# Placing the last edge rows in full columns: 26 scatters of 128 rows and one of 64, where there were 32 of 106

## Time and profile before

| | us |
|---|---|
| timed runs, median of 3 | 4679.84 (4676.11 to 4682.98) |
| profiled execution: span from first to last instruction | 6104.5 |
| GpSimd busy | 3187.4 (52% of the span) |
| TensorE busy | 3504.6 (57%) |
| VectorE busy | 2563.8 (42%) |
| ScalarE busy | 1503.7 (25%) |
| mean granted TensorE clock | 0.746 of full speed |

### The profile page before, as it was taken

One profiled execution on the slowest core, in us unless ns is written; L12 is line 12 of the kernel. 1 busy time (PEld: TensorE's weight loads), 2 busy tenths in 40 slices (PEclk: granted clock), 3 DMA queues, 4 the chain that ended last, 5 costly groups with the idle time before them and its releaser, 6 DMA issues.

```text
span 6104.5 us, 83728 instructions
## 1 busy us (share of the span) xinstructions
PE 3504.6 (57%) x18191; PEld 1755.8 (29%) x18192; DVE 2563.8 (42%) x7891; ACT 1503.7 (25%) x3741; POOL 3187.4 (52%) x3191
## 2 busy tenths in 40 slices
PE   5377777777777777776324544345365345455347
PEld 2133333333333333333101222112132112222136
DVE  6266666666666666666330020131120021120368
ACT  3133333323323232322211111111111112111158
POOL 2455555555555555555376555645625635626720
PEclk8588888878888887888656676667666667667679
DMA  5333333333333333333123444334324334324256
GB/s 181 93 77 81 81 78 78 77 80 77 77 77 80 77 77 78 80 77 71 38 93 135 145 146 131 119 112 145 107 79 144 111 132 146 108 79 156 79 200 237
DMA packets 593641, 646.86 MB, mean 106 GB/s; under 512 B 423668, under 2 KB 430418, under 8 KB 587261
## 3 DMA queue, kind: packets, MB, share of 16 engines
q1 hardware_dynamic: 374705, 459.40, 23.2%
q0 software_dynamic: 101760, 110.75, 9.2%
q10 hardware_dynamic: 117068, 75.50, 4.1%
HBM read 451.74 MB, written 190.23 MB: 105 GB/s over the span
## 4 chain that ended last, share of the span: by engine, by line
PE 35%; issue 21%; another core or an unknown queue 21%; DVE 10%; DMA 8%; ACT 2%; POOL 2%; DVEq 1%; SPq 0%; ACTq 0%; POOLq 0%
PE bank L1742 10%; PE bank L1743 7%; PE bank L1823 6%; PE bank L1747 6%; DMA ld_all<-adjacency 3%; DMA rel_table<-ld_all 2%; DMA rel_and_z<-adjacency 1%; DVE hid_T L1305 1%; DMA ld_all<-l_sorted 1%; POOL l_sorted L711 1%; DVE hid_T L1326 1%; DVE hid_T L1584 1%; PE bank L1939 1%; PE bank L1771 1%
## 5 line engine op out<-in xcount | busy, mean ns | idle before, releaser
L711 POOL DMA_INDIRECT l_sorted<-arena,l_pos x1504 | 1539.2, 1023 | 1339.3 <-ACT arena L854 877.4
L686 POOL DMA_INDIRECT ld_all<-rel_table,rel_and_z x1564 | 1545.8, 988 | 1133.0 <-remote 503.2
L1742 PE MATMUL bank<-hid_T 128*128 128x400 f16 x2346 | 965.7, 412 | 672.6 <-issue 539.8
L1743 PE MATMUL bank<-hid_T 128*128 128x384 f16 x2346 | 940.5, 401 | 44.3 <-issue 43.5
L1326 DVE TENSOR_SCALAR hid_T<-count_key,hid_T 128x400 f16<-128x400 int16 x2346 | 592.1, 322 | 754.5 <-remote 526.7
L1823 PE MATMUL bank<-rel_and_z,ld_all 128*128 128x512 fp8e4 (+1 forms) x1872 | 522.3, 414 | 602.9 <-issue 534.1
L1823 PE MATMUL bank<-ld_all 128*128 128x512 fp8e4 (+1 forms) x1950 | 511.4, 420 | 337.4 <-issue 138.4
L1747 PE MATMUL bank<-ld_all,arena 128*32 x4692 | 527.1, 250 | 123.3 <-issue 121.3
L1742 PEld LDWEIGHTS bank<-hid_T 128*128 x2346 | 255.9, 109 | 1157.3 <-issue 1153.9
L774 ACT CAST ld_all<-bank 128x400 fp8e4<-128x400 f32 x391 | 191.1, 489 | 1551.6 <-remote 999.7
L1266 DVE COPY accT<-bank 128x512 f32<-128x512 f32 (+1 forms) x78 | 51.1, 656 | 1215.4 <-remote 797.1
(11 more groups left out here) (289 smaller groups left out, 4103.0 us busy)
## 6 DMA issues: line engine op xcount, KB each, us to landing
ld_all<-adjacency SPq DMA_DIRECT2D x72, 1600.0 KB
rel_and_z<-adjacency SPq DMA_DIRECT2D x72, 1600.0 KB
l_sorted<-zeros SPq DMA_DIRECT2D x147, 424.0 KB
arena<-in_edge_attr SPq DMA_DIRECT2D x195, 256.0 KB
ld_all<-l_sorted SPq DMA_DIRECT2D x33, 1277.5 KB, 6.0
adjacency<-ld_all ACTq DMA_DIRECT2D x391, 100.0 KB
rel_table<-ld_all SPq DMA_DIRECT2D x49, 520.0 KB, 3.6
ld_all<-rel_table,rel_and_z POOLq DMA_INDIRECT x1564
```

Of the source, the lines that this page charges most:

```text
L686: pool.indirect_dma_start(ring[:, c % RING, 0:TW], None, rel_table, bass.IndirectOffsetOnAxis(ap=rel_i[:, c:c + 1], axis=0)).then_inc(s(f" ...
L711: pool.indirect_dma_start(l3_sorted, bass.IndirectOffsetOnAxis(ap=l3_pos[0:parts, n * SB_K + k:n * SB_K + k + 1], axis=0), rows16[q][0:par ...
L1742: pe.matmul(b0[:, 0:w0], low[:, 0:P], pair_hot[q % 2][:, k, 0:w0], start=k == 0, stop=k == CG - 1)
L1743: pe.matmul(b1[:, 0:GW - w0], low[:, P:2 * P], pair_hot[q % 2][:, k, 0:GW - w0], start=k == 0, stop=k == CG - 1)
```

## The change

The rest of 3392 rows is laid out as 26 full columns of 128 rows (3328 rows, 26 per partition) and one column with the last 64 rows on 64 partitions. It is scattered by 27 indirect DMAs (`REST_DMAS`). The two loads of this rest, that of its source indices (by SyncE at the start) and that of its features (by ScalarE), become two loads each: one of 128 partitions and one of 64, of 4 bytes and of 192 bytes per partition. The waits on them count one more, and SyncE's wait for the scatters of the last block counts 27. Copies and splits still treat 32 columns. `block_in` loses a case that it never met.

```diff
-SB_REST = (E - NSB * SB) // SB_K
+REST_K = (E - NSB * SB) // P
+REST_TAIL = E - NSB * SB - REST_K * P
+REST_DMAS = REST_K + 1
...
-            sp.dma_start(l3_pos[0:SB_REST, NSB * SB_K:n_cols], A["src"][NSB * SB:E].rearrange("(p k) -> p k", k=SB_K)).then_inc(s("l3_src_loaded"), 16)
+            rest = slice(NSB * SB, NSB * SB + REST_K * P)
+            sp.dma_start(l3_pos[:, NSB * SB_K:NSB * SB_K + REST_K], A["src"][rest].rearrange("(p k) -> p k", k=REST_K)).then_inc(s("l3_src_loaded"), 16)
+            sp.dma_start(l3_pos[0:REST_TAIL, NSB * SB_K + REST_K:NSB * SB_K + REST_DMAS], A["src"][NSB * SB + REST_K * P:E].rearrange("(p k) -> p k", k=1),
+                         allow_slow_non_contiguous=True).then_inc(s("l3_src_loaded"), 16)
...
                 for q in range(3):
-                    sp.wait_ge(s(f"l3_moved{q}"), 16 * SB_K * (len(range(q, NSB + 1 - EARLY, 3)) + (q < EARLY)))
+                    last = (NSB - EARLY) % 3 == q
+                    sp.wait_ge(s(f"l3_moved{q}"), 16 * SB_K * (len(range(q, NSB - EARLY, 3)) + (q < EARLY)) + (16 * REST_DMAS if last else 0))
...
                 for m in range(NSB + 1 - EARLY):
                     n = m + EARLY
-                    parts, q = P if n < NSB else SB_REST, m % 3
+                    q = m % 3
...
-                    for k in range(SB_K):
+                    for k in range(SB_K if n < NSB else REST_DMAS):
+                        parts = REST_TAIL if n == NSB and k == REST_K else P
                         pool.indirect_dma_start(l3_sorted, bass.IndirectOffsetOnAxis(ap=l3_pos[0:parts, n * SB_K + k:n * SB_K + k + 1], axis=0),
                                                 rows16[q][0:parts, k, :], None).then_inc(s(f"l3_moved{q}"), 16)
...
-                act.wait_ge(s(f"l3_in{m % 3}"), m // 3 * 16 + 16)
+                act.wait_ge(s(f"l3_in{m % 3}"), m // 3 * 16 + (16 if m + EARLY < NSB else 32))
...
                 if block <= NSB:
-                    parts = P if block < NSB else SB_REST
                     act.wait_ge(s("l3_split"), n + 1)
-                    act.dma_start(ea_in[n % 3][0:parts, :, :],
-                                  A["edge_attr_48"][block * SB:block * SB + parts * SB_K, :].rearrange("(p k) d -> p k d", k=SB_K)).then_inc(s(f"l3_in{n % 3}"), 16)
+                    cols = SB_K if block < NSB else REST_K
+                    act.dma_start(ea_in[n % 3][:, 0:cols, :],
+                                  A["edge_attr_48"][block * SB:block * SB + P * cols, :].rearrange("(p k) d -> p k d", k=cols)).then_inc(s(f"l3_in{n % 3}"), 16)
+                    if block == NSB:
+                        act.dma_start(ea_in[n % 3][0:REST_TAIL, REST_K, :], A["edge_attr_48"][NSB * SB + REST_K * P:E, :]).then_inc(s(f"l3_in{n % 3}"), 16)
...
-            v.wait_ge(s("l3_src_loaded"), 32)
+            v.wait_ge(s("l3_src_loaded"), 48)
```

More of the change, by code:

```diff
@@ L66 @@
 ZERO_DMAS = -(-NBK * CAPC * WL // (2 * ZERO_W))
-assert SB_REST * SB_K == E - NSB * SB and NSB == NG // TG and NSB % 3 == 0 and CAP < FRONT
+assert 0 < REST_TAIL < P and REST_K < SB_K and NSB == NG // TG and NSB % 3 == 0 and CAP < FRONT
 assert PIECES == AHEAD_Z + 4 * (NG // TG) and FULL - PIECES * 8 == 2
@@ L537, in block_in @@
                 n = m + EARLY
-                parts = P if n < NSB else SB_REST
-                sp.dma_start(ea_in[m % 3][0:parts, :, :],
-                             A["edge_attr_48"][n * SB:n * SB + parts * SB_K, :].rearrange("(p k) d -> p k d", k=SB_K)).then_inc(s(f"l3_in{m % 3}"), 16)
+                sp.dma_start(ea_in[m % 3], A["edge_attr_48"][n * SB:(n + 1) * SB, :].rearrange("(p k) d -> p k d", k=SB_K)).then_inc(s(f"l3_in{m % 3}"), 16)
             for a in range(6):
```

## The result

The changed kernel took 4649.8 us (median of 4, 4644.9 to 4652.2), the kernel before on the same occasion 4681.4 (4 runs, 4676.1 to 4685.1): a ratio of 0.9932 with a 95% interval of 0.9918 to 0.9946, or 31.6 us less, between 25 and 38. Forecast were 4655 and 25.1 less, with a gain of 19 to 27 in the main case.

A forecast was written before the change was run, and what follows sets the result against it. GpSimd was taken to set the pace of the timed runs, its last scatter block delaying the last stage; 59.4 us of scatters became 34.3, other parts nothing, so 4679.8 - 25.1 = 4655, range 4650 to 4664.

The forecast's parts named there:

- main case: The forecast itself: shorter last scatter block saves 19 to 27 us, giving 4653 to 4661 us; chance 0.76.
- 1.27 a column: GpSimd's price of a 128-row scatter with its 0.30 us pause, against 1.855 for 106 rows; assumed for 64 rows too.
- 34.3, gain 25.1 on the path: Last scatter block on GpSimd: 59.4 us go, 33.0 and one 64-row scatter come, making 34.3, gain 25.1.
- replay: Last block replayed in the profile's placement, under VectorE's chain: loads at 5823, 22 us sooner, or 19 with a gap.
- GpSimd is nearly always busy: Six adjacency passes in timed runs: GpSimd works 4582 us, leaving about 98 for waits, so TensorE waits for it.
- the last block starts after VectorE has finished: End of the passes in timed runs: VectorE done within 60 to 78 us, GpSimd needs 81 and more before the last block.
- (a): Last block meets VectorE's chain but is not held by it: gain 14 to 17 us, about 4665; chance 0.08.
- (b): Last block beside VectorE's chain, only the old slower scatter form held: gain 38.8 us, time 4641; chance 0.06.
- Rival (c): The 1.55 us scatter price belongs to the last block, not 106 rows: gain 9.3 us, time 4670.5; chance 0.05.
- Rival (d): Slower: the start's load of 64 single words is dear, 10 us together, then about 4690; chance 0.03.
- first load about 14 to 17 us behind the end of VectorE's chain instead of 39: Sign expected in the profile after: the last stage's first load follows VectorE's chain by 14 to 17 us, not 39.
- Rival (e): No change at all, since VectorE holds the last stage in timed runs; chance 0.02.

The follow-up runs named there:

- experiment 4: Kernel before the change, its block of 106-row scatters placed 21st of 47 instead of last; ratios 1.0062 and 1.0060 (long), 4682.6 us, ratio 1.0000 (short).
- experiment 6: Changed kernel with VectorE's large two-input instructions issued as four quarters; 6050.5 us, ratio 0.9999 (long), then 4598.5 us, ratio 0.9819 (short).
- experiments 2: Changed kernel with five extra full-column scatters into a spare tensor in the last block; ratios 1.0044 and 0.9992 to the kernel before, both long.
- experiment 3: Changed kernel with the last edges as 30 columns of 112 rows and one of 32; ratios 1.0047, 1.0000 and 1.0006, all long.
- experiment 5: Kernel before the change, unchanged, profiled again; 4681.2 us against 4680.5, ratio 1.0002 (short).

## Why the prediction was right, and where it was not

The sign, the mechanism and the order of size held: 59.4 us of 106-row scatters gave way to 34.

- **"1.27 a column", 26 full columns and the tail:** the trace has 26 at 0.97 with 0.30 between them, and the 64 rows at 0.90. The price "in no row", taken as 1.27 with 0.6 kept for the other side, was 1.20 with its 0.30. The new block takes 34.0; the forecast 34.3 holds one 0.30 more, behind the last scatter.
- **"34.3, gain 25.1 on the path":** this is the term that was mis-sized. The old block was put at 32 by 1.855 = 59.4, but it has the gap of 3.35 us where 0.30 was counted, and takes 62.1. The prediction saw the gap and counted it in its replay, but not in the sum. The landing is in the replay only, "3.0 later as now", and that does not hold for the new form: it is 1.33 us from the end of the last scatter to the load, against 3.03. With 3.0 from the gap and 1.7 from the landing, 25.1 becomes the 29.8 measured between the two traces. That and the timed 31.6 lie above the 19 to 27 us of the main case. The timed interval, 25 to 38, holds 25.1 as well as 29.8, so the times alone could not have shown the two missing terms.
- **"GpSimd is nearly always busy":** right in what it says of the timed runs. The budget of 4582 us left at most 98 for its waits, and the short trace has 32.3 for ScalarE. Much of the rest is holding: 63 us of it were carried over from the long trace, and the short one has 120 (busy 1596.0 in all, less 1472 by 0.969 and 32 by 1.552). Experiments 4 and 6 show what follows from it. But the reason was wrong: the stalls of the long trace are "mostly gone" because that execution was of another kind, not because nobody recorded.
- **"the last block starts after VectorE has finished":** it started 47 us after (4308.14 to 4355.13), more than the few us that the sum was sure of. Nothing held it, and rivals (a) and (b), which need it beside the chain, could not arise.
- **Rival (c), "the 1.55 us belong to the last block":** ruled out by experiments 2 to 4: 0.97 for 128 rows in the last block, 1.54 for 106 rows in the middle.
- **Rival (d), the start; and "SyncE's 5.93 us issue gone":** not gone. The 128-row load at that place takes 6.51 us, where the 106-row one took 5.93 and, in the second trace of before, 6.42. So the price was never that of 106 rows. The 64 words take 0.57:

```profile
19.32 6.51 SPq L390 DMA_DIRECT2D l_pos<-in_src  x1
25.87 0.57 SPq L391 DMA_DIRECT2D l_pos<-in_src  x1
26.48 3.12 SPq L395 DMA_DIRECT2D arena<-in_edge_attr  x4
```

  The loads behind it go at 26.48 instead of 25.60 and 25.76. The prediction put the edit between 5 us saved and 0.4 lost and at nothing for the time. It was 0.7 to 0.9 lost on that queue, and nothing in the times points to a cost of it.
- **"first load about 14 to 17 us behind the end of VectorE's chain instead of 39":** wrong for either kind. In the short one it is 85 us behind (4306.26 to 4391.11), in the long one right on it (5744.90 to 5745.22).
- **Rival (e), no change, VectorE holding the last stage:** this is what the nine long traces of the experiments show. The forecast took the timed median as its base and is right for that kind. It did not know of two kinds, and it was luck that the occasion gave the short one: on a long occasion the same forecast would have failed.
- **The packets:** the counts here are 80 packets for 106 rows and 32 for each of the others, and the prices are 1.55 us and 0.86 to 0.97. The Trainium skill (DMA: Bandwidth & Descriptors, "Why a DMA increments its semaphore by 16 and not by 1") makes 106 rows use 2 of 16 engines, and 128, 112, 64 and 32 rows all 16. Counts and prices fall into the same two groups; how many engines took part is not shown. Whether divisibility by 16 is the whole of it stays open: no run had a second count of rows that 16 does not divide.

What was not settled is where the gap comes from. It stood in front of the 19th scatter of the 106-row block in all five traces that have one, at the end of the program or in its middle: 3.28 and 3.35 us in the two traces of before, 3.34 in experiment 4's short one, 6.70 and 6.69 in its two long ones. In these traces and in those of the other kernels, no block of another form has a gap in that place. And the timed effect of experiments 2 and 3 in a short execution was not obtained.

## What to carry to other kernels

Price a DMA that GpSimd issues by its form, not by its bytes: 106 rows cost 0.58 us more than 128, so look at the price before sharing a remainder out evenly; here full columns and one short one of 64 rows were cheaper. When one engine's issue sets the pace, a us of it is about a us of the program wherever it lies, and what holds that engine is worth a look: here cutting VectorE's long two-input instructions gave 53 us, the remainder 32. Before a trace is used for a sum, compare its span with the timed median. If they differ by a fifth, the waits and the order of events in it may not be those of the timed runs.

## What the runs showed of the hardware that was not expected

- **Two lengths of one program.** It takes 4680 or 6060 us, one of the two throughout an occasion (35 executions of before within 5988 to 6122 on one), whichever kernel, profiled or not. The chip alone does not decide it: one chip ran before at 4680 us in experiment 5 and at 6080 in the third run of experiment 3. In the long kind TensorE is granted less clock, a mean of 0.754 of 2.4 GHz in the changed kernel against 0.852, but that is not all: its matmuls stand apart without any wait that the profile names. The same group of matmuls in the changed kernel, short and then long (busy us, mean ns, idle before):

```profile
L1830 PE MATMUL bank<-rel_and_z,ld_all 128*128 128x512 fp8e4 (+1 forms) x1872 | 410.4, 379 | 69.8 <-DMA rel_and_z<-adjacency 69.7
```
```profile
L1830 PE MATMUL bank<-rel_and_z,ld_all 128*128 128x512 fp8e4 (+1 forms) x1872 | 525.0, 417 | 577.9 <-issue 526.3
```

  The long one has 526 us of idle time with no releaser (nothing that the profile shows ended it), where nearly all idle time of this group in the short one is a wait for data. No run here tells the cause.
- **A scatter under a two-input VectorE instruction on 128x3328 f32 is held past that instruction's end,** one scatter for each instruction. The one at 4261.77 ends at 4265.53, 0.85 us after the instruction at 4261.06 has ended; the one at 4297.45 ends at 4302.72, 2.05 us after the one at 4297.05, since a one-input instruction of 1.89 us follows that one directly. That makes 3.35 to 5.3 us instead of 0.97. It is not the two inputs alone: the one-input instruction at 4230.90 (TENSOR_SCALAR, 1.89 us) holds the scatter at 4231.08 for 2.56 us, while reductions of 3.6 us hold none. The Trainium skill (SBUF — State Buffer, "Who interferes with whom") tells of a probe in which a two-input instruction did not stall DMA issue. The trace disagrees: 121 us are lost to holding after the change, and experiment 6 gave 53 us back, with 62 us of holding left.
- **A 106-row scatter lands later too.** From its end to the load that waits for it are 3.03 us, against 1.33 for the 64-row one and 1.40 for a full column at the end of experiment 4.
